# Linear attention in an audio tower: inverse and solve on 64x64 diagonal array tiles in place of full-height tiles with half-zeroed operands

## What is computed

```python
def step(S, inp):
    r_t, dec_t, k_t, v_t, kk_t, a_t = inp
    b_t = kk_t * a_t
    sa = jnp.einsum('bvk,bk->bv', S, -kk_t)
    S = S * dec_t[:, None, :] + sa[:, :, None] * b_t[:, None, :] + v_t[:, :, None] * k_t[:, None, :]
    o_t = jnp.einsum('bvk,bk->bv', S, r_t)
    return (S, o_t)
tm = lambda z: jnp.swapaxes(z, 0, 1)
S0 = jnp.zeros((b, d, d), x.dtype)
_, o = jax.lax.scan(step, S0, (tm(r), tm(decay), tm(k), tm(v), tm(kk), tm(a)))
```

## Time and profile before

| | us |
|---|---|
| median of 3 runs | 324.62 |
| lowest, highest | 324.13, 326.79 |
| profiled execution | 324.94 |
| its span, first to last instruction | 322.7 |
| TensorE (PE) busy | 301.4 |
| ScalarE (ACT) busy | 201.6 |
| VectorE (DVE) busy | 198.1 |
| GpSimd (POOL) busy | 140.6 |

### The profile page before, as it was taken

The page is one execution under the profiler, slowest core; times in us unless marked ns, Lnnn a source line. Parts: engine busy times, 40 slices in busy tenths (PEclk is TensorE's granted clock), DMA queues, the critical chain, the costliest instruction groups (busy, mean ns, idle before and its releaser), DMA issues. The chain is left out here.

```text
span 322.7 us, 12475 instructions
## 1 busy us (share of the span) xinstructions
PE 301.4 (93%) x5240; PEld 199.2 (62%) x5240; DVE 198.1 (61%) x414; ACT 201.6 (62%) x385; POOL 140.6 (44%) x142
## 2 busy tenths in 40 slices
PE   3998999999999899999989696999999998999996
PEld 1544566666785654545334165777798998975584
DVE  4467798879853685343576757788896575243202
ACT  1667665445546687787898855669861716675631
POOL 9314799990400006657553249690269610011000
PEclk9999999999999799999999879999999999999999
DMA  7922222222101222222220000000000000000001
GB/s 247 398 61 63 61 60 59 62 61 62 30 4 54 60 60 59 58 65 60 58 59 1 0 2 2 4 2 4 5 2 4 6 4 4 4 5 2 25 2 71
DMA packets 20559, 14.92 MB, mean 46 GB/s; under 512 B 2328, under 2 KB 19352, under 8 KB 20376
## 3 DMA queue, kind: packets, MB, share of 16 engines
q1 hardware_dynamic: 20504, 14.13, 13.9%
HBM read 13.38 MB, written 0.74 MB: 44 GB/s over the span
## 5 line engine op out<-in xcount | busy, mean ns | idle before, releaser
L762 PE MATMUL PS<-arena,K 128*64 128x360 f32 (+1 forms) x800 | 144.2, 488 | 11.4 <-DVE PS L504 5.3
L762 PE MATMUL PS<-arena 128*45 128x45 f32 (+6 forms) x3456 | 119.2, 224 | 3.8 <-ACT arena L460 1.4
L762 PEld LDWEIGHTS PS<-arena 128*45 128x45 f32 (+3 forms) x3456 | 100.2, 126 | 22.3 <-issue 15.2
L762 PEld LDWEIGHTS PS<-arena,K 128*64 128x64 f32 (+1 forms) x800 | 57.9, 150 | 70.6 <-issue 26.7
L302 POOL TENSOR_TENSOR arena<-arena 128x360 f32<-128x360 f32 x32 | 29.9, 960 | 49.8 <-DVE arena L674 49.8
L674 DVE TENSOR_TENSOR arena<-PS,arena 128x360 f32<-128x360 f32 x32 | 16.9, 532 | 23.5 <-PE PS L762 21.4
L550 DVE TENSOR_TENSOR arena<-PS,arena 128x360 f32<-128x360 f32 x24 | 12.8, 533 | 28.8 <-ACT arena L360 28.8
L381 ACT ACTIVATE arena<-arena 128x360 f32<-128x360 f32 x32 | 15.9, 514 | 17.8 <-DVE arena L592 17.4
L402 ACT ACTIVATE arena<-PS,K 128x720 f32<-128x720 f32 x32 | 25.2, 865 | 2.9 <-PE PS L762 2.4
L291 POOL TENSOR_TENSOR arena<-arena,K 128x360 f32<-128x360 f32 x32 | 24.2, 799 | 0.0
L762 PEld LDWEIGHTS PS<-K,arena 128*45 128x45 f32 (+3 forms) x456 | 17.2, 127 | 5.6 <-issue 1.9
(11 more groups left out here) (124 smaller groups left out, 388.3 us busy)
## 6 DMA issues: line engine op xcount, KB each, us to landing
WG<-wr SPq DMA_DIRECT2D x64, 64.0 KB, 1.9
arena<-wr SPq DMA_DIRECT2D x64, 64.0 KB, 1.8
arena<-xT SPq DMA_DIRECT2D x4, 368.0 KB, 5.4
K<-consts SPq DMA_DIRECT2D x1, 1171.0 KB, 10.3
K<-consts SPq DMA_DIRECT2D x1, 852.0 KB, 8.1
out<-arena SPq DMA_DIRECT2D x4, 180.0 KB, 1.9
K<-consts SPq DMA_DIRECT2D x1, 510.0 KB, 6.2
K<-consts SPq DMA_DIRECT2D x1, 352.0 KB, 6.7
```

The source lines that it names most:

```text
L762: return nc.tensor.matmul(o, l, r, start=start, stop=stop)
```

## The change

The matmuls of vt, lx, lt, u, y2, z, w and o take both operands from the partitions of sequence j alone: 64 rows for vt, 45 for lx, lt, u, y2 and o, the first 32 tokens for z and the last 13 (32 to 44) for w. The outputs stay where they were. With that the half-zeroed copies fall away: ScalarE's `m` (L455), one of two evictions of `vt` (L460), its `lt` part at the last level (L469, L473) and its `w` part (L487); VectorE's `lx` writes 360 columns instead of 720 (L734) and its second instruction of `w` (L749) goes. z's eviction is a plain copy. The semaphores ltb, ttb, lt32 and sab fall away with their waits. The level masks have half the columns, `row32` and six columns of `vecs` go. Y moves from slot 3 to slot 5. The core of the diff:

```diff
-     ("negm1T", T), ("eye2", 2 * T), ("levels", len(LEVELS) * 2 * T), ("row32", 1)],
+     ("negm1T", T), ("eye2", 2 * T), ("levels", len(LEVELS) * T)],
...
-M4_, L_, TT_, U_, Y_ = slot(11), slot(9), slot(3), slot(19), slot(3)
-
-KR_ = slot(1)
-X_, VT_, LT_, TB_, SA_ = ((slot(5), slot(7)), (slot(1), slot(17)), (slot(10), slot(15)),
-                               (slot(5), slot(7)), (slot(5), slot(19)))
+M4_, L_, TT_, U_, Y_ = slot(11), slot(9), slot(3), slot(19), slot(5)
+KR_, X_, VT_ = slot(1), slot(5), slot(1)
...
-                elif name == "m":
-                    act.wait_ge(sem["m_ev"], n)
-                    p0, p1 = i * PP // 2, (i + 1) * PP // 2
-                    for j in range(2):
-                        last = s.activation(pair(a(c, LT_[j]))[:, p0:p1], m2(c)[:, p0:p1], ACT.Copy, scale=vec(f"tok{j}"))
-                    last.then_inc(sem["ltb"], 1)
                 elif name == "vt":
                     act.wait_ge(sem["vt_mm"], n)
-                    for j in range(2):
-                        last = s.activation(a(c, VT_[j], 512), bank(c, 0, 512), ACT.Copy, scale=vec(f"tok{j}"))
-                    last.then_inc(sem["vt"], 1)
+                    s.copy(a(c, VT_, 512), bank(c, 0, 512)).then_inc(sem["vt"], 1)
...
-                elif name == "lt" and i == len(LEVELS) - 1:
-
-                    act.wait_ge(sem["t_ev"], n)
-                    for j in range(2):
-                        last = s.activation(pair(a(c, TB_[j])), a(c, TT_, 2 * W).rearrange(
-                            "q (p u t) -> q p u t", u=2, t=T)[:, :, 1, :], ACT.Copy, scale=vec(f"tok{j}"))
-                    last.then_inc(sem["ttb"], 1)
-                    for j in range(2):
-                        last = s.activation(pair(a(c, LT_[j])), m2(c), ACT.Copy, scale=vec(f"early{j}"))
-                    last.then_inc(sem["lt32"], 1)
...
-                    act.wait_ge(sem["ttb"], n)
                     act.wait_ge(sem["y_mm2"], n)
                     s.copy(a(c, Y_, 512), bank(c, 1, 512)).then_inc(sem["y_ev"], 1)
                 elif name == "z":
                     act.wait_ge(sem["z_mm"], n)
-                    s.activation(a(c, U_, 512), bank(c, 0, 512), ACT.Copy, scale=k("row32")).then_inc(sem["z_ev"], 1)
-                elif name == "w":
-                    act.wait_ge(sem["sa"], 2 * n - 1)
-                    s.activation(a(c, SA_[0], 512), a(c, Y_, 512), ACT.Copy, scale=vec("tok0")).then_inc(sem["sab"], 1)
+                    s.copy(a(c, U_, 512), bank(c, 0, 512)).then_inc(sem["z_ev"], 1)
...
                 elif name == "lx":
                     dve.wait_ge(sem["x_mm"], n)
-                    x = a(c, X_[0], 2 * (X_[1] - X_[0])).rearrange("q (j w) -> q j w", j=2)[:, :, 0:W]
-                    level = k("levels", 2 * i * T, 2 * (i + 1) * T).rearrange("q (j t) -> q j t", j=2)
-                    v.tensor_tensor(x.rearrange("q j (p t) -> q j p t", t=T),
-                                    pair(bank(c, 0)).unsqueeze(1).broadcast_to([128, 2, PP, T]),
-                                    level.unsqueeze(2).broadcast_to([128, 2, PP, T]), ALU.mult).then_inc(sem["x_ev"], 1)
+                    v.tensor_tensor(pair(a(c, X_)), pair(bank(c, 0)), over_pairs(k("levels", i * T, (i + 1) * T)),
+                                    ALU.mult).then_inc(sem["x_ev"], 1)
...
                     v.tensor_tensor(a(c, Y_, 512), a(c, Y_, 512), bank(c, 1, 512), ALU.subtract).then_inc(sem["sa"], 1)
-                    dve.wait_ge(sem["sa"], 2 * n - 1)
-                    v.tensor_scalar(a(c, SA_[1], 512), a(c, Y_, 512), vec("tok1"), None, ALU.mult).then_inc(sem["sa"], 1)
...
+            def seq(j, lo=0, hi=T):
+
+                return 64 * j + lo, 64 * j + hi
+
+            def m4(c, p, u, rows):
+                return a(c, M4_ + (4 * p + u) * T, T, *rows)
+
+            def tt(c, p, u, rows):
+                return a(c, TT_ + (2 * p + u) * T, T, *rows)
...
-                        last = mm(to_bank(c, 0, D, j, p, T), a(c, slot(6) + p * T, T), k("Wvf", 64 * j, 64 * j + 64))
+                        f = seq(j, 0, D)
+                        last = mm(to_bank(c, 0, D, j, p, T), a(c, slot(6) + p * T, T, *f), k("Wvf", 64 * j, 64 * j + 64, *f))
...
-                        last = mm(to_bank(c, 0, T, j, p, T), a(c, LT_[j] + p * T, T), tt(c, p, 0))
+                        last = mm(to_bank(c, 0, T, j, p, T), m4(c, p, 2, seq(j)), tt(c, p, 0, seq(j)))
...
-                                last = mm(to_bank(c, 1, T, j, p, T), a(c, X_[j] + p * T, T), tt(c, p, 1))
+                                last = mm(to_bank(c, 1, T, j, p, T), a(c, X_ + p * T, T, *seq(j)), tt(c, p, 1, seq(j)))
...
-                        last = mm(to_bank(c, 0, D, j, p, T), m4(c, p, 0), a(c, VT_[j] + p * D, D))
+                        last = mm(to_bank(c, 0, D, j, p, T), m4(c, p, 0, seq(j)), a(c, VT_ + p * D, D, *seq(j)))
...
-                        last = mm(to_bank(c, 1, D, j, p, T), a(c, TB_[j] + p * T, T), a(c, U_ + p * D, D))
+                        last = mm(to_bank(c, 1, D, j, p, T), tt(c, p, 1, seq(j)), a(c, U_ + p * D, D, *seq(j)))
...
-                        last = mm(to_bank(c, 0, D, j, p, T), a(c, LT_[j] + p * T, T), a(c, Y_ + p * D, D))
+                        early = seq(j, 0, 32)
+                        last = mm(to_bank(c, 0, D, j, p, T), m4(c, p, 2, early), a(c, Y_ + p * D, D, *early))
...
-                        last = mm(to_bank(c, 1, D, j, p, T), a(c, TB_[j] + p * T, T), a(c, U_ + p * D, D))
+                        late = seq(j, 32, T)
+                        last = mm(to_bank(c, 1, D, j, p, T), tt(c, p, 1, late), a(c, U_ + p * D, D, *late))
...
-                    pe.wait_ge(sem["sab"], n)
-                    pe.wait_ge(sem["sa"], 2 * n)
+                    pe.wait_ge(sem["sa"], n)
...
-                                          a(c, (SA_, VT_)[u][j] + p * D, D), m4(c, p, (3, 1)[u]), start=(u == 0),
+                                          a(c, (Y_, VT_)[u] + p * D, D, *seq(j)), m4(c, p, (3, 1)[u], seq(j)), start=(u == 0),
```

More of the change, by code:

```diff
@@ L26 @@
 GROUPS = [
-    [("tokA", 64), ("tokB", 64), ("mean", 128), ("cent", 128), ("vecs", 36)],
+    [("tokA", 64), ("tokB", 64), ("mean", 128), ("cent", 128), ("vecs", 30)],
     [("wq", 128), ("wqr", 128), ("wk", 128), ("wkr", 128), ("wv", 2 * NKV * HD), ("cosq", T), ("sinq", T),
@@ L47 @@
         "eps_ln", "eps_gn", "zero", "ten_ln2", "mix0", "mix1", "mix2", "mix3", "mix4", "mix5", "eidx", "shared",
-        "cw_mid", "cw_low", "rb_mid", "rb_low", "feat0", "feat1", "tok0", "tok1", "tok", "early0", "early1"]
+        "cw_mid", "cw_low", "rb_mid", "rb_low", "tok"]
 H_, N_ = 0, W
@@ L77 @@
 kk bt0 bt tk kp kt kr1 krr krb bon0 bon_mm bon vt_mm vt vd_hi
-m_mm m_ev lv1 tt1 ltb ttb lt32 sab x_mm x_ev t_mm t_ev u_mm u_ev y_mm2 y_ev z_mm z_ev w_mm sa o_mm o_ev
+m_mm m_ev lv1 tt1 x_mm x_ev t_mm t_ev u_mm u_ev y_mm2 y_ev z_mm z_ev w_mm sa o_mm o_ev
 gn_a bonb gn_g ro_mm h3 f_mm f_relu r_mm r_relu fo_mm fo out_done""".split()
@@ L954, in _ @@
                         pe.wait_ge(sem["tt1"], COUNT["m", 1, c])
-                        pe.wait_ge(sem["ltb"], COUNT["m", 1, c])
                         pe.wait_ge(sem["vt"], COUNT["vt", 0, c])
@@ L967, in _ @@
                             for j in range(2):
-                                last = mm(PS[64 * j:64 * j + T, 2 * c + p // 4, lo:lo + T], tt(c, p, 1),
-                                          a(c, X_[j] + p * T, T))
+                                last = mm(PS[64 * j:64 * j + T, 2 * c + p // 4, lo:lo + T], tt(c, p, 1, seq(j)),
+                                          a(c, X_ + p * T, T, *seq(j)))
                             for j in range(2):
                                 last = mm(PS[64 * j:64 * j + T, 2 * c + p // 4, lo + T:lo + 2 * T],
-                                          a(c, X_[j] + p * T, T), tt(c, p, 1))
+                                          a(c, X_ + p * T, T, *seq(j)), tt(c, p, 1, seq(j)))
                         else:
                             for j in range(2):
-                                last = mm(to_bank(c, 1, T, j, p, T), a(c, X_[j] + p * T, T), tt(c, p, 1))
+                                last = mm(to_bank(c, 1, T, j, p, T), a(c, X_ + p * T, T, *seq(j)), tt(c, p, 1, seq(j)))
                     last.then_inc(sem["t_mm"], 1)
@@ L1073, in shape_constants @@
     z["eye2"] = np.concatenate([r == t, r == t], 1)
-    z["levels"] = np.concatenate([(r // (2 * b) == t // (2 * b)) & (r // b > t // b) & (r < T) & (q[:, None] // 64 == j)
-                                  for b in LEVELS for j in range(2)], 1)
-    z["row32"] = r >= 32
+    z["levels"] = np.concatenate([(r // (2 * b) == t // (2 * b)) & (r // b > t // b) & (r < T) for b in LEVELS], 1)
     out = {n: np.asarray(x, np.float32) for n, x in z.items()}
@@ L1128 @@
     cst["b2"], cst["Rb"] = b2, rb
-    vecs = np.zeros((128, 36), np.float32)
+    vecs = np.zeros((128, 30), np.float32)
```

(3 more changed lines are left out.)

8 lines of the change are left out of this document (removed).

## The result

| | before | after |
|---|---|---|
| median | 324.59 us (14 runs) | 327.56 us (14 runs) |
| profiled execution | 324.94 us | 327.45 us |
| its span | 322.7 us | 325.3 us |

The ratio is 1.0084, with a 95% interval of 1.0063 to 1.0104: the changed kernel is 2.7 us (2.0 to 3.4) slower. Three of its 14 runs (332.9 to 334.1 us) fell into a slower state of the chip, and the ratio leaves them out. The difference is within the 1% called "no change" in the prediction (the interval reaches just past it), and the range (323.6 to 329.0) holds the time; but +2.7 lies 1.2 us above the +1.5 forecast, and the median at the upper edge of the 325 to 327.5 that the forecast has for itself.

A forecast was written before the change was run, and what follows sets the result against it. TensorE's own instruction stream was taken to bound the kernel, with the copies beside its work. +2.6 (changes) - 0.8 (streaming) - 0.3 (waits) = +1.5 us, giving 326.1 us by the median, 326.4 profiled; range 323.6 to 329.0.

The forecast's parts named there:

- The wait of o.0:2: Between y2.0:3 and o.0:2, o no longer waits for the half-zeroed copies of L487: 0.2 us won.
- the GpSimd chains: Chains at 194.5 to 201.3 and 237.3 to 243.5 us; GpSimd perhaps slightly faster beside an emptier VectorE, 0.1 us taken.
- the two changes around gg.0:3: Near 229 us, two added tile-shape changes lie under the y2 eviction that releases z: cost 0.
- the price and the count of changes: Matmul steps from 191 us: 33 more tile-shape changes, 20 counted as exposed, at 0.13 us each: +2.6 us.
- Rival A: Every change is paid, the dense stretch covers nothing, no streaming gain: +3.8 us, 328.4 us; chance 0.25.
- the dense stretch: 251 to 273.4 us: 2.1 us lost to late instructions cover most changes; 3 of 12 taken as exposed.
- the prediction's own sign: Stretch 251 to 273 us keeps its length within 0.6 us; growth by 1.6 means every change is paid.
- C: Rival: TensorE with a quarter of its array at work gets a lower clock: +20 us, 345; chance 0.05 with D.
- D: Rival: the two tiles of a diagonal pair take turns: +51 us, 376; chance 0.05 together with C.
- the streaming term: 45-column records of lx and lt go from 0.47 to 0.45 ns a column: -1.3 us, -0.8 taken.
- The step that failed: Compared m's 0.44 ns a column on 64-row tiles with lx's 0.47 on 128 rows: diagonal tiles stream at least as fast.
- The term of the constants: Constants shrink by 187 columns in loads that land long before: 0.

The follow-up runs named there:

- e4: Changed kernel with one unused constants column and its matmuls reading all 128 rows (128x64 tiles, copies gone, values not the reference's): 325.68 us, ratio 1.0025 to before.
- e6: Changed kernel with unused constants columns that put the shared weights and work area back at their old addresses: 326.92 us, ratio 1.0056 to before.
- e3: Kernel before with all half-zeroed copies kept, but matmuls reading only the rows of their own sequence: 327.12 us, ratio 1.0072 to before.
- e7: Changed kernel at its old addresses, with 26 block-diagonal steps also on 64x64 diagonal tiles: 325.08 us, ratio 1.0004 to before.
- e8: Changed kernel at old addresses, 28 block-diagonal steps plus z and w on 64x64 tiles, kept right by a copy and row mask: 323.69 us, ratio 0.9966 to before.
- e1: Changed kernel with one unused constants column, so the shared weights start at column 5428 instead of 5427: 328.39 us, ratio 1.01 to before.
- e9: Kernel before with 12 changes of tile shape put inside six batches of the dense stretch alone: 0.0 us (-0.8 to +0.8), ratio 1.0001.

## Why the prediction was right and where it was wrong

**Right: what bounds the kernel, and that the copies are worth little.** e4 without them is not faster, and e6 lies about 0.5 us below e3, where the prediction had 0.3. The wait of o.0:2 went from 0.26 to 0.05 us as computed (0.2), the GpSimd chains became 0.1 us shorter each, and z.0:0's wait swallowed the two changes around gg.0:3.

**Right: the price and the count of changes.** 0.13 us, between batches, inside them, and for 32-row tiles. e3, e6, e7 and e8 bear it out. e6, which has the changes and not the stall, is +1.8 us (1.2 to 2.4), and the forecast's +1.5 lies in it; but that closeness is in part luck, since the forecast holds 0.8 us of streaming gain that did not come and 0.6 us of changes too many, and the two nearly cancel. Rival A (all are paid, +3.8) is outside the intervals of e6 and of the changed kernel. That the dense stretch kept its length to 0.1 us is luck too: by the prediction's own sign (a growth of 1.6 makes A right) e1's profile, with 1.7, would have spoken for A.

**Right: no loss of clock, no turns.** The granted clock stayed full through the solve and m's pace stayed, which leaves C and D without ground. (One reading was off: of the slices where the clock fell before, the 24th, at 0.7, had TensorE busy 9 tenths, not 6.)

**Wrong: the streaming term, -0.8, was 0.** The step that failed divides 0.68 us by 1440 columns of lx and sets the 0.47 against m's 0.44, as though rows made the difference. Where no shape changes, an lx took 0.64 us from its first record to its last before and 0.64 after. The difference between m and lx is not one of rows. What is left is that lx has the shorter records, which no run here tests by itself. The four 360-column records, on 128 rows and at 0.43 ns a column, stood beside them and spoke against it: rows and record length were both different, and I put it on the rows. The Trainium skill (TensorE: Matmul & The Clock Gate, Step-by-step: what each phase is for) says of the weight load that its time goes by the weights' columns and that the number of rows does not matter, and of the matmul that it goes by the columns streamed. For the two together every run here agrees, 0.64 us a batch of lx on 128 rows and on 45.

**Right in kind, the size open: the dense stretch.** Of 12 changes I took 3 as paid (+0.4). The profiles have -0.1 (after), +0.3 (e3, e6) and +1.7 (e1), mean +0.6; e9, with 12, measured 0.0 (-0.8 to +0.8). The other -0.3 us of difference lie behind it, where 10 changes gave about +1.0 instead of +1.3: in before, batches there followed waits that took some of them in (z.0:2, 0.39 to 0.21 us).

**Wrong: "in loads that land long before: 0".** The term of the constants was costed by their transfer. What they did was move the operands of another engine, +0.83 us in the trace and +0.9 by the runs. "GpSimd's chains changing length, on which I put nothing" was the right place to name but the wrong instruction: the two chains kept their length (0.1 us shorter), and the additions behind them grew. The streaming term and this one are errors of one sign, +0.8 and +0.8; the changes, forecast 0.6 too high, are one of the other. Together they make the 1.1 us by which the profiled execution (327.45) lies above its forecast (326.4), and without the last it would have been about 1.7.

The Trainium skill (TensorEngine Tiling (Array Packing), Gotcha 1) says that row tiles at different places can't access the same bank of PSUM at once. Here the two tiles of every diagonal pair write one bank, and lx, lt, z and w keep the pace that they had as column tiles of 128 rows, where the two of a pair overlap in time (seen in bf16, in the trace of before: two records of 360 columns on column tiles take as little as 0.15 us together, one on the full width 0.16 to 0.17). Taking turns would have cost them half their pace, so the measurement decides against the rule, for this form of fp32 matmul. The Trainium skill (TensorEngine Tiling (Array Packing), Key Properties) says that a change of tiling mode drains TensorE. The traces price a change at 0.10 us, and 0.03 us in the batch behind; that it is a drain they do not show.

## What to carry to other kernels

Here TensorE hardly idled and executed as many records without the zero-padded operands as with them, and taking the copies away was worth about 0.5 us by the nearest comparison; what counted was how often neighbouring batches differ in tile shape. So choose the shape for the neighbours: putting block-diagonal steps and z and w on the same square tiles as the steps beside them turned +1.8 us into -1.1. When a diff changes the size of a packed array, check the durations of untouched instructions first; pad it to the old size to separate the two effects.

## What the runs showed of the hardware

- A change of TensorE's tile shape costs 0.10 us until the next record starts and 0.03 us in the batch behind, whether from 128x64 to 64x64, to 32x64 or back; two of them inside a batch cost 0.21 to 0.27 us.
- Rows are free: records of 45 columns take as long on 45 as on 128 rows, records of 360 as long on 64 as on 128, records of 64 as long on 32 as on 45.
- GpSimd's 128x2048 fp32 addition took 3.8 to 3.9 us with one operand at its original address and 4.5 to 4.7 us with it 4 or 8 bytes further (or 744 to 748 bytes lower, the other operand moved as well).
- VectorE's mix of 128x360 elements takes 0.59 us alone; in after and e1, one that meets a running GpSimd addition or level step ends 0.39 us after it, having taken up to 1.29 us.
- In a stretch of short matmuls about 2 us in 20.7 go to gaps that no wait explains (20.1 to 21.5 us from profile to profile). 12 changes of shape put there cost 0.0 us (-0.8 to +0.8) where 1.6 would be paid, and 36 cost 2.7 (1.7 to 3.7) instead of 4.7.
